# Feed-forward and retention of four batches in one interleaved block, in halves of time, and the retention's weights prepared while the constants load

## The reference

```python
x = x + _L0_attn_a_ref(_layernorm(x), ...)   # norm, conv, selective scan (16 states), gate
x = x + _L0_ffn_ref(_layernorm(x), ...)      # dense ffn + 2 chosen experts of 8
x = x + _L0_attn_b_ref(_layernorm(x), ...)   # retention scan, then softmax attention
x = x + _L0_ffn_ref(_layernorm(x), ...)      # the same ffn again
```

```python
def step(M, inp):
    g_t, k_t, v_t, q_t = inp
    M = g_t[..., None, None] * M + k_t[..., None] * v_t[..., None, :]
    h = jnp.einsum('bhd,bhde->bhe', q_t, M)
    return (M, h)
```

## Time and profile before

| | us |
|---|---|
| median of 3 runs | 1385.68 |
| lowest, highest | 1381.11, 1390.2 |
| the profiled execution, time | 1391.36 |
| its span, first to last instruction | 1389.4 |

### The profile page before, as it was taken

How to read it: one execution, slowest core, us unless ns; L and a number is a source line. 1 busy time by engine, 2 the same in 40 slices (tenths; PEclk the granted TensorE clock), 3 DMA queues, 4 the chain that set the end, 5 groups by cost and what they waited for, 6 DMA issues and landing times. The chain is left out here.

```text
span 1389.4 us, 17492 instructions
## 1 busy us (share of the span) xinstructions
PE 1071.3 (77%) x5850; PEld 393.9 (28%) x5850; DVE 742.7 (53%) x1012; ACT 975.3 (70%) x884; POOL 325.7 (23%) x194
## 2 busy tenths in 40 slices
PE   4748777777799956777446888888888888679996
PEld 3213333333344422332341111111111111134443
DVE  5869998987566648998481001200300300256664
ACT  3767665754688832221336999999999999658885
POOL 3117776766111114665100000000000000011110
PEclk8769999999899978998777999999999999879998
DMA  2000100100100000000001111111111111000002
GB/s 73 0 16 30 31 30 30 60 30 31 32 30 30 31 24 0 0 0 1 8 0 33 24 24 32 37 24 28 22 33 34 24 24 28 11 31 31 30 30 61
DMA packets 24188, 36.48 MB, mean 26 GB/s; under 512 B 7362, under 2 KB 11970, under 8 KB 24130
## 3 DMA queue, kind: packets, MB, share of 16 engines
q1 hardware_dynamic: 24130, 35.71, 9.5%
HBM read 16.82 MB, written 6.29 MB: 17 GB/s over the span
## 5 line engine op out<-in xcount | busy, mean ns | idle before, releaser
L1674 ACT ACTIVATE att_prob<-att_s_ps 128x1536 f32<-128x1536 f32 x342 | 459.2, 1912 | 7.4 <-PE att_s_ps L1588 7.3
L1603 PE MATMUL att_o_ps<-att_prob,att_va 128*32 128x512 f32 x2048 | 273.9, 607 | 0.5 <-ACT att_prob L1674 0.5
L1705 DVE COPY att_o_sb<-att_o_ps 128x512 f32<-128x512 f32 x32 | 22.1, 691 | 381.7 <-PE att_o_ps L1603 381.7
L1588 PE MATMUL att_s_ps<-att_q_st,att_k_st 32*128 32x512 f16 x1024 | 134.4, 388 | 80.8 <-ACT att_prob L1674 76.1
L685 POOL TENSOR_TENSOR scan_hc<-scan_state,scan_c_rep 128x1024 f32<-128x1024 f32 x64 | 151.9, 2392 | 71.9 <-DVE scan_state L642 71.7
L787 POOL TENSOR_TENSOR ffn_veps<-ffn_mv,all_eps 128x4 f32<-128x4 f32 x16 | 9.1, 570 | 575.3 <-DVE ffn_mv L944 575.3
L642 DVE TENSOR_TENSOR_SCAN scan_state<-scan_decay,scan_drive_ps 128x1024 f32<-128x1024 f32 x64 | 142.9, 2270 | 0.3 <-ACT scan_decay L615 0.3
L282 PE MATMUL scan_y_ps<-scan_hc,all_ident 128*128 128x512 f32 x256 | 130.2, 634 | 8.3 <-DVE scan_y_sb L661 6.2
L1588 PEld LDWEIGHTS att_s_ps<-att_q_st,att_k_st 32*128 32x128 f16 x1024 | 33.1, 91 | 327.2 <-ACT att_prob L1674 315.9
L619 ACT ACTIVATE scan_c_rep<-scan_c_ps 128x1024 f32<-128x1024 f32 x64 | 65.4, 1022 | 80.4 <-PE scan_c_ps L282 80.1
L1012 DVE SCALAR_TENSOR_TENSOR ffn_hid_lo<-ffn_hid,ffn_share,ffn_hid_hi 128x1024 f16<-128x1024 f32 x64 | 81.9, 1283 | 48.8 <-ACT ffn_hid_hi L920 48.1
(11 more groups left out here) (215 smaller groups left out, 1505.8 us busy)
## 6 DMA issues: line engine op xcount, KB each, us to landing
ffn_w_sel<-w_split SPq DMA_DIRECT2D x16, 512.0 KB, 3.2
w_split<-scan_w_parts SPq DMA_DIRECT2D x8, 512.0 KB, 2.9
att_q_st<-hv_part SPq DMA_DIRECT2D x64, 64.0 KB, 2.1
att_k_st<-hv_part SPq DMA_DIRECT2D x64, 64.0 KB, 2.1
ln_x_half<-in_x SPq DMA_DIRECT2D x8, 256.0 KB, 2.8
scan_w_raw<-in_w1e SPq DMA_DIRECT2D x8, 256.0 KB, 3.2
scan_w_raw<-in_w2e SPq DMA_DIRECT2D x8, 256.0 KB, 3.4
out<-store_out SPq DMA_DIRECT2D x8, 256.0 KB, 2.4
```

Source lines behind the costliest of these rows:

```text
L1588: last = pe.matmul(s_ps[e % 2][:, n, :], k_st[rows, g % 2, kc * P:(kc + 1) * P], q_st[rows, g % 2, HALVES[half]], start=True, stop=True)
L1603: last = pe.matmul(o_ps[half][32 * j:32 * j + 32, :], va[:, g % 2, kc, j, :], prob[:, (GH * v + j) % RING, :], start=kc == 0, stop=kc == K ...
L1674: act.activation(prob[:, first % RING:first % RING + n, :], s_ps[e % 2][:, 0:n, :], ACT.Exp).then_inc(exped.sem, 1)
```

## The change

`ffn` and `retention` are gone. In their place stands `mixture(t, name, jobs, rets)`, one block for the feed-forward of the batches `jobs` and the retention of the batches `rets`. It is called once with all four batches for both (in `group`, which also calls `queries_and_keys` and `attention`), and once after the attention with jobs alone. All of it is written out, with no hardware loop, along steps s. Every instruction is 512 columns wide:

- Step s does `up(s)`, `down(s - 2)`, gelu, cast and residue of one half chunk. A batch has RUN = 24 steps: its 12 chunks for the first half of time, then for the second. The feed-forward ends at step 95.
- The norms of batches 1 to 3 begin at steps 1, 9 and 17, those of the retention at 25, 49, 73 and 97, each over some 13 steps, all through one `a_ps` and one `z_ps` of 512 columns. x is transposed from `t.x_t` directly, with no copy `x_half`.
- The k, g, q, v products of a retention batch come at its norm's step + 6 to + 13, one half each (`make`, `take`). The 16 half units follow from + 8 on, three steps for two units, for the last batch one each step (`unit_slot`). Steps run on to 137; the last unit is at 120.
- The gate is 0.5 + 0.5 tanh(x / 2) instead of the sigmoid; the output is scaled by ScalarE, per half; head sums go into `sum_ps`, which the choice of experts uses too.

Elsewhere: `load_constants` also loads all weights of the retention and of queries, keys and output, makes the f16 parts of the retention's weights, the temperature, `a_neg` and the output bias. `queries_and_keys` reads `t.h_seq` with no copy. `selective_scan` and `scan_inputs` are written out, `dt_b` is gone, the weight splits come at steps 1, 4, 7, ... 25 of 64. Each stage's semaphores are cleared by POOL when the stage is left (they are used again).

```diff
@@ Stage.__exit__
+        nums = sorted(sem.num for sem in self.sems)
+        for first in (n for n in nums if n - 1 not in nums):
+            end = next(n for n in range(first, first + len(nums) + 1) if n not in nums)
+            self.nc.gpsimd.sem_clear(range(first, end))
@@ load_constants
+                sp.dma_start(w_all[:, 0:len(RET_MATS), :], d["ret_mats"]).then_inc(ret_loaded, 16)
+                sp.dma_start(w_all[:, len(RET_MATS):W, :], d["wsv"]).then_inc(ret_loaded, 16)
+                sp.dma_start(t.head_sum[:, :, :], d["head_sum"]).then_inc(att_loaded, 16)
...
                 sp.wait_ge(loaded, 16 * 4)
+                sp.wait_ge(ret_loaded, 16 * 2)
+                sp.wait_ge(att_loaded, 16 * 4)
...
+                act.wait_ge(ret_loaded, 16 * 2)
+                act.activation(t.ret_hi[:, :, :], w_all[:, :, :], ACT.Copy, scale=WS).then_inc(ret_high, 1)
...
+                dve.wait_ge(ret_high, 1)
+                dve.scalar_tensor_tensor(t.ret_lo[:, :, :], w_all[:, :, :], WS, t.ret_hi[:, :, :], ALU.mult,
+                                         ALU.subtract)
@@ selective_scan
-        SPLITS = (3, 11)
+        SPLITS = tuple(1 + 3 * k for k in range(E + 1))
@@ mixture
+    RUN = 2 * M
+    UNITS = 2 * HD
+    FIRST = -1
+    norm_at = [(FIRST, "ffn", 0)] + [(1 + 8 * i, "ffn", i + 1) for i in range(N - 1)]
+    norm_at += [(RUN + 1 + RUN * r, "ret", r) for r in range(R)]
...
+    def unit_slot(r, w):
+        return norm_at[RET_Q[r]][0] + 8 + (3 * w // 2 if r + 1 < N else w)
...
+            kv_ps = [ps(f"kv_ps{k}", [P, HALF]) for k in range(2)]
+        h_ps = [ps(f"h_ps{k}", [P, HALF]) for k in range(2)]
+        o_ps, a_ps, z_ps, sum_ps = (ps(n, [P, HALF]) for n in ("o_ps", "a_ps", "z_ps", "sum_ps"))
@@ mixture, PE
+                def up(s):
+                    i, half, m, k, c = place(s)
+                    if m == 0:
+                        pe.wait_ge(z_rest.sem, z_rest.at(i, half))
+                    if k and c == 0:
+                        pe.wait_ge(e_loaded[k - 1], 16 * (i + 1))
+                    if s >= 2:
+                        pe.wait_ge(gelued.sem, gelued.at(0, s - 2))
...
+                def key_value(r, w):
+                    h, n = divmod(w, HD)
+                    if r or w >= 2:
+                        pe.wait_ge(scanned.sem, scanned.at(r, w - 2))
...
+                for h in range(2):
+                    turn_x(0, "ffn", 0, h)
+                    turn_z(0, h)
+                gate(0, 0)
+                for s in range(LAST + 1):
+                    if s < RUN * N:
+                        up(s)
...
+                    if 0 <= s - LAG < RUN * N:
+                        down(s - LAG)
...
+                    for r, p in products_at(s):
+                        make(r, p)
+                    for r, w in units_at(s):
+                        key_value(r, w)
+                    for r, x in sums_at(s):
+                        add_heads(r, x)
@@ mixture, ScalarE
+                for s in range(LAST + 1):
+                    if s >= M + LAG and (s - LAG) % M == 0 and s - LAG <= RUN * N:
+                        output(s - LAG - 1)
+                    if s < RUN * N:
+                        gelu(s)
...
+                    for r, p in products_at(s):
+                        take(r, p)
@@ mixture, VectorE
+                for h in range(2):
+                    statistics(0, h)
+                    normalise(0, h)
+                    low_part(0, "ffn", 0, h)
...
+                for s in range(LAST + 1):
+                    if s < RUN * N:
+                        rest(s)
...
+                    for r, w in units_at(s):
+                        outer(r, w)
+                        if w:
+                            scan(r, w - 1)
@@ queries_and_keys
-                def stage_h(b):
-                    act.wait_ge(made.sem, made.before(b, 1, 2))
-                    act.activation(h_b[:, :], t.h_seq[:, b, :], ACT.Copy).then_inc(h_staged.sem, 1)
@@ attention
-                sp.dma_start(t.wo[:, :], t.dram["wo"]).then_inc(wo_loaded, 16)
@@ hybrid_layer
-        ffn(t, "ffn1")
-        with Stage(nc, "hv") as s:
...
-        ffn(t, "ffn2")
+        group(t, batches, [], [])
+        mixture(t, "mix4", batches, [])
```

More of the change, by code:

```diff
@@ L359, in _ @@
                 pe.wait_ge(wbc_ready, 32)
-                with pe.Fori(0, B - 1) as b:
+                for b in range(B - 1):
                     for_u(b + 1)
@@ L396, in _ @@
                 silus(0)
-                with act.Fori(0, B - 1) as b:
+                for b in range(B - 1):
                     copy_x1(b + 1)
@@ L452, in _ @@
                                 pick[:, :].rearrange("p (n o) -> p n o", o=1).broadcast_to([BC3, 2 * NS, P]))
-                with dve.Fori(0, B - 1) as b:
+                for b in range(B - 1):
                     convolve(b + 1)
@@ L571, in body @@
                 def body(b, n):
-                    more = there(b, n, NS)
+                    more = there(b, n, NS, N)
                     if more:
@@ L753, in ffn, with weight_of_expert, place @@
[L753 to L761 removed]
+        def weight_of_expert(i, k):
+            return share[:, i, k - 1:k] if k else t.blend[:, 0:1]
+        def place(s):
+            i, m = divmod(s, RUN)
+            half, m = divmod(m, M)
+            return i, half, m, *divmod(m, FC)
@@ L792, in body @@
-                def body(b, last):
-                    if not last:
-                        for k in range(2):
-                            deviation(b + 1, k)
-                    pool.wait_ge(y_made.sem, y_made.at(b))
-                    pool.sem_inc(seen, 1)
-                    pool.tensor_tensor(t.x_t[:, b, :], t.x_t[:, b, :], y[:, :], ALU.add).then_inc(added.sem, 1)
-                for k in range(2):
-                    deviation(0, k)
-                with pool.Fori(0, B - 1) as b:
-                    body(b, False)
@@ new lines, in _ @@
+                for h in range(2):
+                    deviation(0, h)
+                for s in range(LAST + 1):
+                    if s >= M + LAG and (s - LAG) % M == 0 and s - LAG <= RUN * N:
+                        add(s - LAG - 1)
+                    for q, kind, i in norms(s, 0):
+                        deviation(q, 0)
+                    for q, kind, i in norms(s, 3):
+                        deviation(q, 1)
+                    for r, w in units_at(s):
+                        if w:
+                            weigh(r, w - 1)
+                    for r, w in units_at(s - 1):
+                        if w == UNITS - 1:
+                            weigh(r, w)
@@ L1337, in queries_and_keys @@
+def queries_and_keys(t, batches):
+    nc, d = t.nc, t.dram
+    N = len(batches)
+    with Stage(nc, f"qk{batches[0]}") as q:
         raw = q.sb("raw", [P, 2, TT, P])
@@ L1389, in _ @@
                 project(0)
-                with pe.Fori(0, B - 1) as b:
-                    project(b + 1)
+                for b in range(N):
+                    if b + 1 < N:
+                        project(b + 1)
                     turn(b)
-                turn(B - 1)
             @block.scalar
```

1157 lines of the change are left out of this document (504 added, 653 removed).

## The result

The changed kernel takes 1441.86 us (median of 4 runs, 1440.03 to 1443.55), the kernel before 1385.51 on the same chip: ratio 1.041, 95% interval 1.037 to 1.044. It is slower, as forecast, but by 56 us where 18.5 were forecast, and 10 us above the top of the range. The profiled execution has a span of 1441.4 us against 1389.4, so 52.0 us are to be explained. Both traces are divided at the same events: the first product of the scan stage, the last residual addition of the scan, the last copy of the head sums, the last low part of queries and keys, the last addition of attention, the last addition of the second feed-forward.

What follows compares the result with a forecast made beforehand. VectorE bounds the scan; feed-forward (PE) and retention (VectorE) want different engines, 321.6 us together. Terms 7 + 0.5 + 16.5 + 6 - 11 - 0.5 = +18.5 gave 1404 us for the median, range 1394 to 1420.

Steps and rivals of the forecast that it cites:

- the scan stage: Unrolled scan with splits every three steps: 0 us, bounds -4 and +4, as POOL and ScalarE have room on average.
- The second feed-forward: Last block, mixture without retention: +6 us, bounds -1 and +13, of which prologue +4.
- batch 0's 43 us: Second feed-forward's first 24 slots, holding three later norms: 38 us of VectorE work, about 43 with waits.
- The first block: Mixture with retention: four pieces, 16 + 57 + 181 + 84 = 338 us against 321.6, +16.5, bounds -27 and +50.
- The ring: Mixture's middle: closed loop scan, product, up, gelu, cast, residue, outer, next scan; 6.9 us per three slots.
- One sign: Mixture: VectorE waits for the cast and a unit's product, 1.3 us or more per three slots.
- the extras put on the ring: Mixture slots 33 to 96: retention norms 11, q, k, g, v products 5 per batch, head sums 11, lower clock 7 us.
- Tail: Mixture from slot 97, norm and 21 units without feed-forward: 3.3 us per unit, 84 us, bounds 74 and 92.
- Constants: Loading stage: +7 us, bounds +5 and +9; next stage's first DMA near 11.7 us, waiting for the wide weights.
- Prices of halves: 512-wide instructions: gelu with cast 1.33 us, residue and outer product 0.67 each in pitch, scan 1.12, 1.20 to its end.
- the first: Rival: queues overlap well, VectorE alone limits; block 289 us, time 1355; faster than the half-way case, chance 0.20.
- The third: Rival: PE starves and its clock falls through the mixture too, half the middle slow; about 1432 us, chance 0.15.

Runs made afterwards that it cites:

- both ways of removing the one wait: Changed kernel with weight splits every seven steps instead of three, 1406.5 us; or every three with two buffers each for enlarged weights and parts, 1407.5 us.
- the norms drawn out: Changed kernel with splits every seven steps, scan(w) directly behind outer(w), and later norms spread over more slots (VectorE normalises two slots behind statistics): 1367.6 us.
- The scan at once: Changed kernel with scan(w) directly behind outer(w) on VectorE, GpSimd's weighing reordered likewise: 1416.6 us, ratio 1.024.
- the run with the ring closed: Changed kernel without GpSimd's weighing of memory by queries, its scan order kept; head sums read the memory itself, output not the reference's: 1430.3 us.

## Why the prediction was right in direction and wrong in size

**The step that failed is the scan stage**, "0, bounds -4 and +4". It measured +28.4, more than half of the whole loss, and both ways of removing the one wait gave 30 us or more back (247.3 and 248.7 us, inside the bound of -4). The prediction read the averages of the earlier trace rows, GpSimd 170.6 and ScalarE 154.4 of 251.1 us busy, concluded "both have room", and even wrote "some scans wait". What it did not do is what it did for the mixture: ask which instruction waits for which buffer, and what is queued behind. Enlargement k waits for low part k-1. At three steps' distance ScalarE's lead over GpSimd is longer than the distance. In eight such meetings ScalarE waited 41.6 us, and 28 us of it reached VectorE. With this wait taken away the kernel takes 1406.5 us, near the forecast's 1404; that it is so near is luck, for the other misses below partly cancel.

**The second feed-forward**, +6 forecast, +16.1 measured. The prologue was right: 14.3 us from block start (1255.56) to first product (1269.88) against 10.3, so +4. The later batches were right (33.5 forecast, 34.4 and 33.7). The mis-sized term is batch 0's 43 us: its 24 slots took 50.1. I had filled them with 38 us of VectorE's work and allowed 5 for waits. In fact each norm held the slots up for 5.4 us. With the norms drawn out the same 24 slots took 43.4. From the first product to the first residue it was 4.2 us instead of 3, which is most of the rest.

**The first block**, 338 forecast, 333.9 measured, was near by errors that cancel. Prologue to the first residue 18.1 against 16. Slots 0 to 32: 71.2 against 57, mostly the same mis-sized norm, here four of them (61.9 with the norms drawn out). Slots 33 to the last residue: 170.7 against 181, but these are 62 slots, and the forecast counts 64. The ring itself was right: 6.91 us for three slots where no weighing disturbs it, against 6.9, and 7.15 where one does; and 68.3 and 66.9 us per 24 slots against 66 to 68. One sign did not come, VectorE's waits of 1.3 us or more per three slots: they were 0.52, because the residue made longer by GpSimd fills them. What was too dear there were the extras put on the ring. Of the clock's 7 us that is seen, for in the middle the granted clock was 0.98; how the rest divides is not shown. Tail, counted from the last residue: 74.0 against 84. The unit was right, 2.80 and 3.43 us against 2.75 and 3.4, at both clocks. I had taken 3.3 for all, but about half of the tail ran at the full clock (0.75 granted in the window above, against the low clock throughout that the forecast leaned on), and the last extras were counted too high. The bounds given for the block, -27 and +50, do not follow from those of its pieces either, which add up to -32 and +48. Two scans at the low clock:

```profile
676.82 0.39 PE L883 MATMUL mix_kv_ps<-mix_z_hi,all_ret_hi 128*128 128x512 f16 x1 [1.97 <-DVE mix_mem L1152]
...
678.09 0.76 DVE L1140 SCALAR_TENSOR_TENSOR mix_kv_ps<-mix_kv_ps,all_bsv_large,mix_k_sb 128x512 f32<-128x512 f32 x1 [1.32 <-PE mix_kv_ps L883]
678.76 1.21 DVE L1152 TENSOR_TENSOR_SCAN mix_mem<-mix_g_sb,mix_kv_ps 128x512 f32<-128x512 f32 x1
...
681.52 0.76 DVE L1140 SCALAR_TENSOR_TENSOR mix_kv_ps<-mix_kv_ps,all_bsv_large,mix_k_sb 128x512 f32<-128x512 f32 x1 [1.56 <-PE mix_kv_ps L883]
682.19 1.21 DVE L1152 TENSOR_TENSOR_SCAN mix_mem<-mix_g_sb,mix_kv_ps 128x512 f32<-128x512 f32 x1
```

**Constants**, +7: the first x DMA went out at 10.99 (11.7 forecast, 4.75 before), and the input norms ended 6.8 us later (35.8 against 28.9). So the wait for the weights was near what was forecast, though the forecast let the temperature hide under it, and without it the temperature shows. But the scan's first product came only 4.5 us later: the stage between took 66.3 instead of 68.7 us. Its loops are written out in the change, which I did not cost. That this is the cause is not shown: in the runs with this part unchanged the first product came anywhere between 98.9 and 102.4 us, a wider spread than the 2.4 us in question.

**Table loads**: none added, as forecast. In both blocks the gelus have one load each, the eight tanh gates none (group by line, changed kernel):

```profile
L999 ACT ACT_TABLE_LOAD x2 | 2.6, 1283 | 0.0
```

**Queries and keys** -11: measured -9.8, the first product of the projection 0.6 us after the last head sum's copy. **Prices of halves** were right where nothing ran beside them (gelu and cast 0.68 and 0.72, outer 0.75, scan 1.21). **The rivals**: the first (VectorE alone the limit, 1355) did not come about in this kernel. The scan at once was not enough for it, 24 slots still took 64 us; it needed GpSimd's weighing out of the way too, and then they took 58. The third gave nearly the measured time, 1432, but for a reason that is absent: the clock in the middle was 0.98.

## What to carry to other kernels

Where a side job is interleaved into a pipeline, its average load says nothing. Write down for each of its steps which buffer it waits for, how far its engine runs ahead of the one that frees it, and what stands behind it in the queue. If the spacing of two jobs is less than that lead, each meeting costs a wait; here eight of them cost 28 us. And when an order closes a loop over three engines, try first the order in which the consumer follows its producer at once: here it gave 24 us, and the next limit showed itself only then.

## What the runs showed of the hardware

A VectorE pass and a GpSimd pass can hold each other up. VectorE's residue (both tensors in SBUF, 512 columns) took 0.75 us in the median and up to 1.84 us where GpSimd worked beside it, and GpSimd's weighing 1.27 in the median and up to 1.82. The outer product (0.73 to 0.76) and the scan (1.20 to 1.27), which read one of their tensors from PSUM, never showed it. Without the weighing the expert residues were all at 0.72 to 0.75. One meeting that was left there, in the run with the ring closed, GpSimd then VectorE:

```profile
510.72 1.27 POOL L1216 TENSOR_TENSOR all_x_t<-all_x_t,mix_y 128x512 f32<-128x512 f32 x1
```

```profile
511.11 1.43 DVE L1127 SCALAR_TENSOR_TENSOR mix_hid_lo<-mix_hid,all_blend,mix_hid_hi 128x512 f16<-128x512 f32 x1
```

The residue is issued 0.39 us into GpSimd's addition and ends at 512.54, 0.55 us after the addition's end at 511.99: it seems to have stood still until then. The other way round, VectorE then GpSimd, in the changed kernel:

```profile
563.74 0.72 DVE L1127 SCALAR_TENSOR_TENSOR mix_hid_lo<-mix_hid,mix_share,mix_hid_hi 128x512 f16<-128x512 f32 x1
```

```profile
563.90 1.69 POOL L1225 TENSOR_TENSOR mix_qm<-mix_mem,mix_q_sb 128x512 f32<-128x512 f32 x1 [3.92 <-DVE mix_mem L1152]
```

The residue keeps its time, and the weighing, 1.27 us long where nothing overlaps it, ends 1.13 us after it, at 565.59. In the changed kernel every residue that overlaps a weighing or an addition of the output by more than 0.05 us does one of these two: either it ends 0.55 us after GpSimd's pass, or GpSimd's pass ends 1.12 to 1.14 us after it. So the two never share, one goes behind the other. The Trainium skill (SBUF — State Buffer, "Who interferes with whom") says that a VectorE instruction with two SBUF inputs contends with a GpSimd instruction that reads SBUF, and one with at most one SBUF input, outside the two-port modes, does not. This case agrees, in both directions, and it cost about 6 us per 24 slots once VectorE was the limit: 88 passes kept VectorE busy for 61.4 us with the weighings and for 54.7 without them (the two windows above, both from 501 us on).

A pass with a single tensor, in SBUF, was held up too: the gate's second pass took 0.40 to 0.42 us alone and 1.48 to 1.50 us where a weighing had begun before it. Here the weighing had begun at 538.58 and ended at 540.27:

```profile
470.81 0.42 DVE L1132 TENSOR_SCALAR mix_g_sb<-mix_g_sb 128x512 f32<-128x512 f32 x1
...
539.07 1.49 DVE L1132 TENSOR_SCALAR mix_g_sb<-mix_g_sb 128x512 f32<-128x512 f32 x1
```

Whether that pass runs in a two-port mode is not shown in these traces.
